# First attention block of a macaron layer: four row loads, normalisation on VectorE, turns by half, filler products placed earlier

## The reference, cut to what matters

```python
x = x + 0.5 * ffn(layernorm(x))            # 8 experts, top-1, capacity 160, D=256, F=1024
x = x + attn(layernorm(x))                 # no softmax: a gated complex scan over the sequence
x = x + 0.5 * ffn(layernorm(x))            # the same experts again

def attn(z):                               # z: (4, 1024, 256)
    q, k, v, g = z @ Wq, z @ Wk, z @ Wv, z @ Wg
    a = z @ Wa                             # real and imaginary half
    a = sigmoid(|a|) * exp(1j * angle(a))
    h = scan(h_t = a_t * h_(t-1) + k_t * v_t)
    y = real((q * h * silu(g)) @ Wo)
    y = layernorm(y + z) * s1 + b1
    return layernorm(gelu(y @ W1 + b1) @ W2 + b2 + y) * s2 + b2
```

## Time and profile before

| | |
|---|---|
| median of 3 runs | 725.93 us (724.41 to 726.29) |
| profiled execution | 726.66 us, of which the span of its instructions is 725.0 us |
| mean granted TensorE clock | 0.947 of full speed |
| TensorE busy | 648.2 us (89%) |
| VectorE busy | 477.0 us (66%) |
| ScalarE busy | 453.9 us (63%) |
| GpSimd busy | 196.6 us (27%) |

### The profile page before, as it was taken

How to read it: one execution, slowest core, us unless ns; L and a number is a source line. 1 busy time by engine, 2 the same in 40 slices (tenths; PEclk the granted TensorE clock), 3 DMA queues, 4 the chain that set the end, 5 groups by cost and what they waited for, 6 DMA issues and landing times. The chain is left out here.

```text
span 725.0 us, 11552 instructions
## 1 busy us (share of the span) xinstructions
PE 648.2 (89%) x4309; PEld 572.3 (79%) x4309; DVE 477.0 (66%) x1056; ACT 453.9 (63%) x815; POOL 196.6 (27%) x292
## 2 busy tenths in 40 slices
PE   8988999686879899999999899999997789799993
PEld 5457999555668889889899799898887689389993
DVE  5661700135697989989989989988989777520001
ACT  3314444037779889888898898898797243244440
POOL 6141011221013123424234234235125131420112
PEclk9997999899879999999999999999999799799997
DMA  6949882150101201202201220211011086117700
GB/s 206 330 161 381 285 289 80 50 166 31 57 29 59 73 1 46 73 1 74 74 19 56 73 69 7 72 44 41 4 44 44 1 296 227 52 37 238 248 23 24
DMA packets 48816, 74.07 MB, mean 102 GB/s; under 512 B 4614, under 2 KB 40539, under 8 KB 48696
## 3 DMA queue, kind: packets, MB, share of 16 engines
q1 hardware_dynamic: 44408, 59.84, 24.8%
q0 software_dynamic: 4352, 13.49, 5.2%
HBM read 62.45 MB, written 15.20 MB: 107 GB/s over the span
## 5 line engine op out<-in xcount | busy, mean ns | idle before, releaser
L1617 PE MATMUL bank<-zt_h,w_in_h 128*128 128x512 f32 x192 | 80.8, 421 | 14.5 <-DVE zt_l L1277 6.1
L982 PE MATMUL bank<-xdt,ring 128*128 128x160 f32 x512 | 78.8, 314 | 4.7 <-issue 3.6
L1617 PE MATMUL bank<-yt_h,w_h 128*128 128x256 f32 x256 | 74.4, 291 | 7.3 <-DVE yt_l L1402 6.3
L982 PEld LDWEIGHTS bank<-xdt,ring 128*128 128x128 f32 x512 | 75.4, 202 | 6.4 <-issue 6.0
L784 DVE SCALAR_TENSOR_TENSOR xo<-bank,gate,xg 128x256 f32<-128x256 f32 x20 | 9.3, 481 | 106.6 <-PE bank L1009 106.6
L1619 PE MATMUL bank<-zt_h,w_in_l 128*128 128x512 f32 x192 | 76.5, 399 | 0.0
L1618 PE MATMUL bank<-zt_l,w_in_h 128*128 128x512 f32 x192 | 76.4, 398 | 0.0
L1617 PE MATMUL bank<-w_h,ht_h 128*128 128x256 f32 x256 | 74.3, 290 | 0.0
L995 PE MATMUL bank<-hid,ring 128*128 128x160 f32 x512 | 72.8, 300 | 1.5 <-DVE idx_s L768 0.7
L1618 PE MATMUL bank<-w_l,ht_h 128*128 128x256 f32 x256 | 72.4, 283 | 0.0
L1619 PE MATMUL bank<-w_h,ht_l 128*128 128x256 f32 x256 | 72.3, 283 | 0.0
(11 more groups left out here) (243 smaller groups left out, 1620.4 us busy)
## 6 DMA issues: line engine op xcount, KB each, us to landing
ring<-in_L_ffn_w SPq DMA_DIRECT2D x32, 1024.0 KB, 10.4
xc<-in_L_attn_x SPq DMA_DIRECT2D x8, 512.0 KB, 4.2
zb<-x_mid SPq DMA_DIRECT2D x8, 512.0 KB, 5.1
z_mid<-zb POOLq DMA_DIRECT2D x8, 512.0 KB, 3.4
zr<-z_mid SPq DMA_DIRECT2D x16, 256.0 KB, 2.9
xr<-x_mid SPq DMA_DIRECT2D x16, 256.0 KB, 3.6
out<-xq POOLq DMA_DIRECT2D x16, 256.0 KB, 4.2
xc<-in_L_attn_W SPq DMA_DIRECT2D x4, 512.0 KB, 5.3
```

The source lines that it names most:

```text
L982: ins = T.matmul(bank[b][:, 0:CAP], w1_of(s)[:, k, m * P:(m + 1) * P], xdt[:, k, e * CAP:(e + 1) * CAP], start=k == 0, stop=k == KD - 1)
L1617: T.matmul(out, left[0], right[0], start=start, stop=False)
```

## The change

Block 0 alone gets its own way to the projections. Its rows are loaded in four transfers of 128 KB with a semaphore each. DVE takes the statistics of a tile when its transfer is in, GpSimd computes no shift, and DVE instead of ACT normalises the four tiles (`norm_rows`: subtract the mean, multiply by `rsz`). TensorE turns all four tiles of half 0 and then those of half 1, and reports each half. The filler products are 30 ahead of the wait for `par_ready`, and 14 behind the first tile's load; they now write `upb[0]`. In every block, the wait of project steps 0 and 3 for `proj_read[1]` stands ahead of the products of `k` = 1 of the first output.

```diff
+        z_tile = [sem(f"z_tile{t}") for t in range(JT - 1)] + [z_in[0]]
@@
-                power(rsz, mvz, "eps_in", JT, zrstd, shz)
+                power(rsz, mvz, "eps_in", JT, zrstd, None if is_first(b) else shz)
@@
-                sp.dma_start(zb[b.par][:], rows).then_inc(z_in[b.par], 16)
+                if is_first(b):
+                    for t in range(JT):
+                        sp.dma_start(zb[0][:, t, :], x_mid[t * P:(t + 1) * P, :]).then_inc(z_tile[t], 16)
+                else:
+                    sp.dma_start(zb[b.par][:], rows).then_inc(z_in[b.par], 16)
@@
             def z_stats(b, j):
+                if is_first(b):
+                    for t in range(JT):
+                        v.wait_ge(z_tile[t], 16)
+                        own.step(V.bn_stats(stz[:, t, :], zb[0][:, t, :]))
+                        if t:
+                            own.after(own.n - (1 if t == 1 else 2))
+                            own.step(V.bn_aggr(mvz[:, t - 1, :], stz[:, t - 1, :]))
+                    own.after(own.n - 1)
+                    V.bn_aggr(mvz[:, JT - 1, :], stz[:, JT - 1, :]).then_inc(zvar, 1)
+                    return
@@
+            def z_norm(b, j):
+                if is_first(b):
+                    v.wait_ge(zrstd, 1)
+                    for t in range(JT):
+                        norm_rows(nc, zb[0][:, t, :], zb[0][:, t, :], mvz[:, t, 0:1], rsz[:, t:t + 1]).then_inc(z_ready, 1)
@@
             def z_norm(b, j):
+                if is_first(b):
+                    return
                 act.wait_ge(zrstd, b.n + 1)
@@
         def _(pe):
             T = nc.tensor
-            pe.wait_ge(par_ready, 1)
...
+            keep_busy(30, upb[0])
+            pe.wait_ge(par_ready, 1)
 
             def z_turn(b, j):
                 if is_first(b):
-                    keep_busy(30)
-                    pe.wait_ge(z_in[0], 16)
-                    keep_busy(12)
+                    pe.wait_ge(z_tile[0], 16)
+                    keep_busy(14, upb[0])
+                    for k in range(KD):
+                        for t in range(JT):
+                            if k == 0:
+                                pe.wait_ge(z_ready, t + 1)
+                            ins = T.transpose(proj[k][:, t * P:(t + 1) * P], zb[0][:, t, k * P:(k + 1) * P], ident[:])
+                        ins.then_inc(proj_ready[k], 1)
+                    return
@@
             def project(b, j):
                 h, i = divmod(j, 3)
-                if i == 0:
-                    pe.wait_ge(proj_read[1], b.n * 7 + (1 + 3 * h))
                 for n in range(2):
                     wait(pe, proj_read[n], b.n * 7 + (1 + 3 * h + i))
                     c = slice((2 * i + n) * D + h * P, (2 * i + n) * D + (h + 1) * P)
                     for k in range(KD):
+                        if i == 0 and n == 0 and k == 1:
+                            pe.wait_ge(proj_read[1], b.n * 7 + (1 + 3 * h))
```

More of the change, by code:

```diff
@@ L1468, in _ @@
             per_quarter = (2 * QT - 1) + (3 * QT - 2) + (3 * QT - 2)
-            run(v, dict(choose=choose, place=half_step, hot=half_step, rows=half_step, z_stats=z_stats, z_low=z_low, fold=fold, size=size,
+            run(v, dict(choose=choose, place=half_step, hot=half_step, rows=half_step, z_stats=z_stats, z_norm=z_norm, z_low=z_low, fold=fold, size=size,
                         denominator=denominator, tangent=tangent, phase=phase, turns=whole, gate=gate,
@@ L1619, in split_matmul, with keep_busy @@
                 return T.matmul(out, left[1], right[0], start=False, stop=stop)
-            def keep_busy(n):
+            def keep_busy(n, to):
                 for _ in range(n):
-                    T.matmul(o_ffn[:], cst["ones_h"][:], cst["iota_p"][:, 0:BT // CT, :].rearrange("p a b -> p (a b)"),
+                    T.matmul(to[:], cst["ones_h"][:], cst["iota_p"][:, 0:BT // CT, :].rearrange("p a b -> p (a b)"),
                              start=True, stop=True)
+            keep_busy(30, upb[0])
+            pe.wait_ge(par_ready, 1)
             def z_turn(b, j):
                 if is_first(b):
-                    keep_busy(30)
-                    pe.wait_ge(z_in[0], 16)
-                    keep_busy(12)
+                    pe.wait_ge(z_tile[0], 16)
[7 more added lines that the diff above has]
+                    return
                 for k in range(KD):
```

## The result

The changed kernel took 720.93 us in the median of 11 runs (718.21 to 725.61), the kernel before 727.06 in 11 runs beside it (724.41 to 728.19): ratio 0.9933, 95% interval 0.9914 to 0.9952, so 4.9 us (3.5 to 6.3) faster by the ratio, which is the measure used below; the two medians lie 6.1 apart. The forecast was 3.8 us faster, 722.1 us.

A forecast was written before the change was run, and what follows sets the result against it. TensorE, busy 89% of the span, was taken to lose most at the serial seam between first expert half and attention. Seam -4.25, moved wait -1.55, clock +2.0 gave -3.8 us: 722.1 us, range 719.7 to 724.6.

The forecast's parts named there:

- full-clock rival: TensorE's clock does not fall behind the seam: 5.8 us faster, 720.1 us; chance 0.22.
- Seam: Between first expert half and attention: block 0's first projections start 4.25 us earlier, between 3.2 and 4.7.
- The load: Block 0's rows in four transfers: last tile in at 145.9 instead of 146.43, a gain of 0.5 us.
- What is late next: VectorE's queue at the seam: six bias operations behind `z_norm` end at 151.8, 1.2 us after ScalarE's first copy.
- The small row: Last small row, issued 1.2 us later, holds block 0's bias operations for 0 to 0.15 us; taken as 0.
- Clock behind the seam: Half clock in block 0's first projections after TensorE's near-idle stretch: 2.0 us lost, from estimates of 1.5 and 2.7.
- Moved wait in blocks 0 to 2: Products run ahead of the `proj_read[1]` wait: gains 0.65, 0.3 and 0.6 us, together 1.55, between 0 and 2.0.
- Moved wait in the loop: Later blocks: gains nothing; what TensorE saves waiting for `qg` it idles waiting for `yo`.
- Tiles one behind the other: Rival: block 0's four transfers run serially, last tile at 151.85; +2.15 us, 728.1 us; chance 0.04.
- The held VectorE: Rival: tiles land no earlier, block 1's late load holds VectorE until `fold` 1 is late; 725.9 us; chance 0.09.

The follow-up runs named there:

- again: The changed kernel run once more unaltered, beside the kernel before: 722.49 us, ratio 0.9948.
- start_only: The changed kernel with the moved wait of `project` undone in every block, leaving only the seam: 722.23 us, ratio 0.9941.
- wait_first: The changed kernel with the moved wait only in blocks 0 to 2, blocks 3 to 7 waiting as before: 720.05 us, ratio 0.9914.
- filled: The changed kernel with 18 instead of 14 fillers behind the first tile and 9 more behind block 0's eight transposes: 722.44 us, ratio 0.9955.
- fill_behind: The changed kernel with the first 30 fillers behind the wait for `par_ready` again: 725.69 us, ratio 0.9966.

## Why the prediction was right

Its sum was 3.8 us and the trace has 3.83 from the load to the last `xo`. But the terms met less well than the total, and that they cancelled so closely is luck. The timed 4.9 us and 3.8 us (again) lie around it; the median of 720.93 is nearer to the full-clock rival's 720.1 than to 722.1, but the traces rule that rival out.

- **Seam: right.** Forecast 4.25, measured 4.48 and 4.05 in two executions. The last `bn_stats` came at +3.70 (forecast 3.65), the power at +4.71 (4.55), the normalised rows at +7.2 (7.5), the bias operations ended at +9.23 (9.55). The power took 1.04 instead of the 1.28 that I carried over from one row. The fillers out of the way and the split load were each confirmed by undoing them (+15.22 and +11.66). The range's lower end was added up wrongly: 4.25 less 0.7, 0.44 and 0.05 gives 3.1, not 3.2.
- **The load: right in size, not in kind.** The prediction took 4.1 us for the landing of the whole, but that is where VectorE started; it landed at 3.73. The 0.5 us that it booked for an earlier landing came from VectorE's start behind it.
- **What is late next: right.** The bias operations were the bound; moving them brought the first projection from +10.0 to +8.8.
- **The small row: undersized.** I allowed 0 to 0.15 us for it and took 0. Of the six traces with this order (changed, again, start_only, wait_first, filled, fill_behind), VectorE waited for it in two: 0.34 us (again) and 0.81 us (filled).
- **Clock behind the seam: right in kind, oversized.** Taken 2.0 (1.5 to 2.7), measured 1.44 and 1.5 for 3.4 us at half clock. The larger price exists: 6.8 us at half clock in the kernel with one load.
- **Moved wait in blocks 0 to 2: right.** Forecast 0.65, 0.3 and 0.6; measured 0.67, 0.68 and 0.61 in the ledger. Block 1 gained twice what I took: I weighed ScalarE's busy time, but TensorE's wait shrank from 3.30 to 2.70 and its products came that much earlier. Of block 2's 0.61, the fall behind the wait of 1.91 us took 0.4 back before the next `yo`.
- **Moved wait in the loop: wrong.** I priced it at nothing, since what TensorE saves at the first wait it idles at the second. That is what happened: the wait for `yo` grew from 0.95 to 1.64. But I stopped there and took idle time off the critical path to be free. With the longer pause the clock fell in one to three blocks of the loop, in every one of the 8 traces with the moved wait. Against it stand 0.1 us per block that the wait does gain. The net is a loss of about 1 us in an execution with one fall, 4 to 5 with three. The sum came out because this loss stood against a seam, a clock and a block 1 that were each a few tenths better than forecast (0.23, 0.56 and 0.38 us).
- **Rivals.** Full clock (720.1): it did not hold in either execution of the changed kernel. Tiles one behind the other: the last of four was in 3.7 us after the first issue. (That rival's +2.15 is 1.7 + 2.0 - 1.55; it counts the moved wait's gain, though its words say "without".) The held VectorE: block 1's statistics did wait 0.84 us for their load, with nothing behind them; block 2's would have become the bound if the rest had been faster, as the run with the late bias operations showed.

The Trainium skill (DMA: Bandwidth & Descriptors, section Anatomy of one DMA) gives a fit from which the prediction estimated 3.2 us for the whole 512 KB and 3.55 for the fourth tile, a loss of 0.35 by the split. The page states that fit for transfers issued from GpSimd, and these were issued by SP. The traces have landings at +3.73 to +3.78 for the whole and at +3.43 to +3.98 for the fourth tile, so there was neither that loss nor a clear gain in landing.

What is not settled: the timed gain of the moved wait alone (4.4 us by its ratio) against nothing in its one trace; and how far timed differences between kernels come from the first expert half, whose end moves by 3.1 us between two executions of the same kernel, and from the second, where three traces took 2.8 us more.

## What to carry to other kernels

Idle time of TensorE off the critical path is not free: two short waits were harmless here where a longer one cost the clock in about half of its occurrences. So price a moved wait by the pauses that it leaves and their chance of a fall, not by their sum alone, and look at the granted clock behind each. When a step moves to an engine because it is faster there, list what was hidden in that engine's queue: here six small operations became the bound, and putting them behind the urgent ones brought the first projection 1.2 us forward, where the move itself had brought at most 0.5. Fillers belong ahead of the wait that they bridge, where they start at full clock and end before the data.

## What the runs showed of the hardware

- Of TensorE's pauses between 250 and 540 us, 11 of the 24 that lasted 1.60 to 1.65 us (TensorE working 2.35 to 2.40 us of the 4 up to their end) were followed by half clock, at least one in each of the 8 traces that have them. None of the 75 that lasted 0.8 to 1.15 us was. A fall lasted 3.4 us there and cost 1.6 to 1.7 us.
- The length of the pause alone does not decide: behind a pause of 1.91 us ahead of the loop the clock fell in 10 of 14 traces and held in 4, the kernel before among them.
- Four loads of 128 KB in a row, issued over 1.34 us, were in 3.4 to 4.0 us after the first issue (11 traces), one of 512 KB after 3.73 to 3.78 us (3 traces), with the same two broadcast loads behind them.
- VectorE's first instruction on the loaded rows, after 6.5 to 8.3 us of idling, started 0.45 us after the landing in all 14 traces, and 0.02 us after it on a later tile for which it had waited 0.3 us or less. Why is not shown.
- A 1 KB row behind two broadcast loads landed at very different times: with the same order of issue, VectorE was held by it for nothing in four traces, for 0.34 us in one and for 0.81 us in one.
